# Table rows by one-hot matmul: one fp32 matmul a chunk in place of two on rounded halves

## The reference

```python
e = jnp.stack([tbl_0[ids[:, 0]], ..., tbl_25[ids[:, 25]]], axis=1)
combined = jnp.concatenate([dense[:, None, :], e], axis=1)
interactions = jnp.einsum('bfd,bgd->bfg', combined, combined)
z = jnp.concatenate([dense, interactions[:, iu, ju]], axis=1)   # iu, ju: 351 pairs
h = jnp.concatenate([z, dense], axis=1)
h = jnp.maximum(h @ W_top1 + b_top1, 0.0)
h = jnp.maximum(h @ W_top2 + b_top2, 0.0)
y = h @ W_top3
```

## Time and profile before

| | us |
|---|---|
| median of 3 runs | 196.87 |
| lowest, highest | 195.58, 198.09 |
| the profiled execution | 195.5 |
| its span in the trace | 193.7 |
| TensorE busy | 113.5 |
| VectorE, ACT, POOL busy | 75.6, 73.3, 66.7 |

### The profile page before, as it was taken

One profiled execution on the slowest core, in us unless ns is written; L12 is line 12 of the kernel. 1 busy time (PEld: TensorE's weight loads), 2 busy tenths in 40 slices (PEclk: granted clock), 3 DMA queues, 4 the chain that ended last, 5 costly groups with the idle time before them and its releaser, 6 DMA issues.

```text
span 193.7 us, 2685 instructions
## 1 busy us (share of the span) xinstructions
PE 113.5 (59%) x1038; PEld 94.6 (49%) x1038; DVE 75.6 (39%) x153; ACT 73.3 (38%) x160; POOL 66.7 (34%) x75
## 2 busy tenths in 40 slices
PE   1699300940004900100009999975799999989995
PEld 0377100720003600100007767765799898979894
DVE  3797314811100500010149799937192262014400
ACT  7864213411003001110035898448194373233512
POOL 3777837777777856777300000000000000000000
PEclk9999955596555765555555999999699999999999
DMA  5487532252211381121102740000000000000000
GB/s 189 131 266 203 169 89 60 53 177 54 56 52 48 83 234 31 53 54 54 41 0 76 250 129 0 0 3 0 12 4 6 8 0 3 0 0 5 3 0 0
DMA packets 6304, 12.58 MB, mean 65 GB/s; under 512 B 2545, under 2 KB 3157, under 8 KB 6163
## 3 DMA queue, kind: packets, MB, share of 16 engines
q1 hardware_dynamic: 3971, 7.68, 13.6%
q0 software_dynamic: 2176, 4.46, 8.6%
q10 hardware_dynamic: 144, 0.26, 0.4%
HBM read 11.27 MB, written 0.00 MB: 58 GB/s over the span
## 4 chain that ended last, share of the span: by engine, by line
PE 50%; another core or an unknown queue 33%; ACT 8%; DVE 3%; issue 3%; DMA 2%; ACTq 0%; DVEq 0%
PE ps L541 10%; PE ps L544 9%; PE ps L602 9%; PE ps L573 9%; PE ps L557 3%; PE ps L615 3%; PE ps L524 2%; ACT emb_t L383 2%; DVE z L487 2%; ACT hot L377 2%; DMA ids_i<-in_ids_dram 2%; PE ps L511 1%; ACT away L369 1%; ACT z L410 1%
## 5 line engine op out<-in xcount | busy, mean ns | idle before, releaser
L342 POOL DMA_INDIRECT rows<-in_tbl_dram,ids_i x68 | 65.9, 969 | 26.9 <-issue 24.2
L541 PE MATMUL ps<-hot,tab_hi 125*128 125x512 f32 x72 | 34.6, 481 | 55.8 <-ACT emb_t L383 55.7
L460 DVE TENSOR_SCALAR hot<-ps,row_no 125x512 fp32r<-125x512 f32 x54 | 37.7, 744 | 67.0 <-remote 39.9
L541 PEld LDWEIGHTS ps<-hot,tab_hi 125*128 125x128 f32 x72 | 17.0, 235 | 62.2 <-ACT emb_t L383 57.1
L544 PE MATMUL ps<-hot,tab_lo 125*128 125x512 f32 x72 | 33.3, 462 | 0.7 <-issue 0.7
L377 ACT ACTIVATE hot<-away 125x512 fp32r<-125x512 f32 x18 | 10.9, 627 | 43.4 <-remote 35.4
L487 DVE COPY z<-ps 32x112 f32<-32x112 f32 (+1 forms) x64 | 16.5, 258 | 15.8 <-PE ps L573 15.0
L410 ACT COPY z<-ps 32x112 f32<-32x112 f32 (+1 forms) x64 | 15.3, 239 | 13.5 <-PE ps L573 12.8
L573 PE MATMUL ps<-emb_t 128*64 128x52 f32 x512 | 17.9, 233 | 3.7 <-ACT emb_t L402 2.2
L573 PEld LDWEIGHTS ps<-emb_t 128*64 128x64 f32 x512 | 17.2, 149 | 5.1 <-ACT emb_t L402 3.1
L544 PEld LDWEIGHTS ps<-hot,tab_lo 125*128 125x128 f32 x72 | 16.8, 233 | 5.0 <-issue 1.2
(11 more groups left out here) (44 smaller groups left out, 77.4 us busy)
## 6 DMA issues: line engine op xcount, KB each, us to landing
tab<-in_tbl_dram SPq DMA_DIRECT2D x9, 448.0 KB
rows<-in_tbl_dram,ids_i POOLq DMA_INDIRECT x68
w_fold<-w_pair SPq DMA_DIRECT2D x1, 1024.0 KB
w<-in_W_top_dram SPq DMA_DIRECT2D x1, 512.0 KB
tab<-in_tbl_dram SPq DMA_DIRECT2D x9, 52.0 KB
x_rows<-in_r_dense_features_dram ACTq DMA_DIRECT2D x1, 256.0 KB, 2.8
w_x<-in_W_top_dram SPq DMA_DIRECT2D x1, 256.0 KB
h_t<-in_W_top_dram SPq DMA_DIRECT2D x1, 256.0 KB
```

The source lines that it names most:

```text
L342: pool.indirect_dma_start(out=rows[:, t, gathered.index(f), :], out_offset=None, in_=tables[f - 1], in_offset=bass.IndirectOffsetOnAxis(id ...
L460: nc.vector.tensor_scalar(hot[0:RP, k % OHB], ps[0:RP, IDV + n % 2, :], row_no[0:RP, c:c + 1], None, ALU.is_equal).then_inc(hot_dve, 1)
L541: nc.tensor.matmul(bank, tab_hi[0:RP, n % SPLIT, c], one_hot, start=c == 0, stop=False)
```

## The change

The one-hots become plain fp32, and a chunk is one fp32 matmul on the loaded table in place of two on its halves. `tab_hi`, `tab_lo`, the cast on ACT and the subtraction on VectorE are gone, and with them two semaphores. TensorE waits for the table's own load (`tab_in`). `tab` has three buffers and the one-hots sixteen; SP loads table n when all eight chunks of table n - 3 have been used. The broadcasts for table n + 2 stand ahead of the last two chunks of table n and no longer behind them.

```diff
--- before.py
+++ after.py
@@ -78,9 +78,8 @@
     ND = 2
     ACT_CHUNKS = (3, 6)
     DVE_CHUNKS = tuple(c for c in range(R8) if c not in ACT_CHUNKS)
-    OHB = 10
-    RAW = 2
-    SPLIT = 2
+    OHB = 16
+    RAW = 3
     gathered = [f for g in GROUPS for f in features(g) if f]
     assert D == P and N1 == BK and sorted(gathered + ONEHOT) == list(range(1, NF))
     assert all(tables[f - 1].shape[0] == R8 * RP for f in ONEHOT) and w1.shape[0] == 2 * D + NPAIR
@@ -162,9 +161,7 @@
         row_no = sb("row_no", [P, R8])
         neg_row = sb("neg_row", [P, R8])
         tab = sb("tab", [P, RAW, R8, D])
-        tab_hi = sb("tab_hi", [P, SPLIT, R8, D], F32R)
-        tab_lo = sb("tab_lo", [P, SPLIT, R8, D], F32R)
-        hot = sb("hot", [P, OHB, B], F32R)
+        hot = sb("hot", [P, OHB, B])
         away = sb("away", [P, 2, B])
         h1_t = sb("h1_t", [P, 2, NB, P])
         w_xb = h1_t[:, 1].rearrange("p c b -> p (c b)")
@@ -201,8 +198,6 @@
         w_x_ready = sem("w_x_ready")
         ids_bc_dve = sem("ids_bc_dve")
         ids_bc_act = sem("ids_bc_act")
-        hi_ready = sem("hi_ready")
-        lo_ready = sem("lo_ready")
         hot_dve = sem("hot_dve")
         away_ready = sem("away_ready")
         hot_act = sem("hot_act")
@@ -272,7 +267,7 @@
             def load_table(n):
                 if n >= RAW:
 
-                    sp.wait_ge(lo_ready, n - RAW + 1)
+                    sp.wait_ge(hot_used, (n - RAW + 1) * R8)
                 lines = tables[ONEHOT[n] - 1].rearrange("(p c) d -> p c d", c=R8)
                 for p0, p1 in ((0, SPREAD), (SPREAD, RP)):
                     sp.dma_start(tab[p0:p1, n % RAW], lines[p0:p1]).then_inc(tab_in[n], 16)
@@ -352,12 +347,6 @@
             nc.scalar.copy(w_pair[:].rearrange("p k n -> p (k n)"),
                            zeros[:].to_broadcast([P, NQ * N1])).then_inc(w_pair_zeroed, 1)
 
-            def split_hi(n):
-                act.wait_ge(tab_in[n], 32)
-                if n >= SPLIT:
-                    act.wait_ge(hot_used, (n - SPLIT + 1) * R8)
-                nc.scalar.copy(tab_hi[0:RP, n % SPLIT], tab[0:RP, n % RAW]).then_inc(hi_ready, 1)
-
             def build_hots(n):
                 act.wait_ge(ids_bc_act, n + 1)
                 if n == 0:
@@ -383,17 +372,13 @@
                 nc.scalar.copy(emb_t[:, :, :, ONEHOT[n]],
                                ps[:, ROT + bank_of(s), :].rearrange("p (t b) -> p t b", t=T)).then_inc(stored_act, 1)
 
-            split_hi(0)
             build_hots(0)
-            split_hi(1)
             for s in steps:
                 if s[0] == "hot":
                     n = s[2]
                     if n + 1 < NH:
                         build_hots(n + 1)
                     store_hot(s)
-                    if n + 2 < NH:
-                        split_hi(n + 2)
                 elif s[0] == "group" and stored_by_act(s):
                     act.wait_ge(group_ps, s[1] * NG + s[2] + 1)
                     copies = list(group_copies(s))
@@ -444,16 +429,9 @@
             nc.vector.tensor_copy(ids_t[:], ps[0:NF - 1, IDV + 1, :]).then_inc(ids_t_ready, 1)
             dve.wait_ge(row_no_ready, 1)
 
-            def split_lo(n):
-                dve.wait_ge(hi_ready, n + 1)
-                nc.vector.tensor_tensor(tab_lo[0:RP, n % SPLIT], tab[0:RP, n % RAW], tab_hi[0:RP, n % SPLIT].bitcast(F32),
-                                        ALU.subtract).then_inc(lo_ready, 1)
-
             def build_hots(n):
                 dve.wait_ge(ids_bc_dve, n + 1)
                 for m, c in enumerate(DVE_CHUNKS):
-                    if m == 2:
-                        split_lo(n)
                     k = n * R8 + c
                     if k >= OHB:
                         dve.wait_ge(hot_used, k - OHB + 1)
@@ -530,21 +508,17 @@
                 if s[0] == "hot":
                     n = s[2]
                     wait_bank(s)
-                    pe.wait_ge(hi_ready, n + 1)
+                    pe.wait_ge(tab_in[n], 32)
                     bank = ps[:, ROT + bank_of(s), :]
                     for c in range(R8):
+                        if c == R8 - 2 and n + 2 < NH:
+                            broadcast_ids(n + 2)
                         if c in ACT_CHUNKS:
                             pe.wait_ge(hot_act, n * len(ACT_CHUNKS) + ACT_CHUNKS.index(c) + 1)
                         else:
                             pe.wait_ge(hot_dve, n * len(DVE_CHUNKS) + DVE_CHUNKS.index(c) + 1)
-                        one_hot = hot[0:RP, (n * R8 + c) % OHB]
-                        nc.tensor.matmul(bank, tab_hi[0:RP, n % SPLIT, c], one_hot, start=c == 0, stop=False)
-                        if c == 0:
-                            pe.wait_ge(lo_ready, n + 1)
-                        nc.tensor.matmul(bank, tab_lo[0:RP, n % SPLIT, c], one_hot,
-                                         start=False, stop=c == R8 - 1).then_inc(hot_used, 1)
-                    if n + 2 < NH:
-                        broadcast_ids(n + 2)
+                        nc.tensor.matmul(bank, tab[0:RP, n % RAW, c], hot[0:RP, (n * R8 + c) % OHB],
+                                         start=c == 0, stop=c == R8 - 1).then_inc(hot_used, 1)
                 elif s[0] == "group":
                     _, t, g = s
                     feats = features(GROUPS[g])
```

## The result

The changed kernel takes 216.37 us (median of 4, 214.04 to 220.81) against 196.66 for the kernel before (now the median of 4). The ratio is 1.089, with a 95% interval of 1.077 to 1.101; it leaves disturbed runs out, and so lies a little under the ratio of the medians. The forecast was 215.2 us. The profiled execution took 214.44 us, with a span of 212.6.

A forecast was written before the change was run, and what follows sets the result against it. Late TensorE counts bound the kernel until about 100 us, then TensorE's own work. Tables +17.8, store and broadcasts +0.5, front 0, last stretch 0: +18.3 on execution 195.5 gives 213.8, plus 1.4 makes 215.2 us; range 204 to 225.

The forecast's parts named there:

- Two regimes: Until about 100 us TensorE's late counts to other engines set the pace; from 101.5 us TensorE's own work does.
- An fp32 chunk at 0.90 us: Tables behind 101.5 us: a chunk grows from 0.455 to 0.90 us, a table by 3.56, five tables by 17.8.
- Rival 4: One-hot matmuls: fp32 costs two passes, a chunk stays at 0.455 us, only the broadcasts' 0.5 counts: 197.4 us; chance 0.06.
- The slow start adds nothing: TensorE from 101.55 us: nearly 5 us of slow passes (0.42 us, not 0.23) recur unchanged, adding nothing.
- The broadcasts at 0.5 us: Broadcasts moved ahead of the last two chunks no longer hide ACT's store: about 0.5 us in all, between 0 and 1.5.
- The front adds nothing: Before 101.5 us: slower first tables are swallowed by a backlog whose end POOL sets; 0, bounds +9 or -9 us.
- paying 4 us a count: Third table, from near 40 us: each of eleven TensorE counts takes 4 us, so its last comes near 83 us.
- Loads and buffers at 0: Later table loads and SP's pair-weight loads stay hidden: 0; if cover is gone, a wait of 2 to 3 us.
- The last stretch at 0: Pair products and dense layers, the last 67.5 us, do not change: 0.
- Rivals 1 and 2: Tables before 101.5 us: front slips, up to +9, 224 us (chance 0.16); or gains a table, 206 us (0.12).
- the forecast's own case: Whole kernel: fifth table starts near 101.6 us as before, five fp32 tables behind it, 215.2 us; chance 0.58.
- Rival 3: TensorE's counts to ACT and VectorE: backlog vanishes, fifth table starts before 83.2 us, 157 us; chance 0.08.

The follow-up runs named there:

- paced gathers: Two small POOL memsets put behind each gather: 157.68 us on the changed kernel, 155.09 on the kernel before; 154.50 on the changed kernel with broadcasts moved back.
- run with short matmuls: Kernel before with two extra 16-column matmuls in each chunk, their results unused: 222.45 and 254.56 us.
- one changed line on POOL: Kernel before with POOL waiting for the group just before, not the one before that, to land ahead of each group of gathers: 158.05 us.

## Why the prediction was right

*Two regimes.* Right, and shown from both sides: with the gathers cut to a quarter, both kernels lose their idle middle, and the change costs 26.3 us in place of 19.7.

*An fp32 chunk at 0.90 us.* 0.870 measured, so a table grows from 3.64 to 6.96 us: +3.3, where the sum had +3.56, and +16.6 for five tables in place of +17.8. Rival 4 (two passes) is out: the records are 0.435 us apart and not 0.23.

*The slow start adds nothing.* Right. The fifth table took 7.41 us to its broadcasts where the sixth took 5.35, 2.1 more; the kernel before lost 2.3 in the same way.

*The broadcasts at 0.5 us.* Mis-sized. The two waits that the move opens are 0.69 and 0.90 us. From the fifth table's start to the seventh's the changed kernel takes 20.3 us and the one before 12.5, 7.8 less; two tables' chunks are 6.6 of it, so the move costs about 1.2. With the hold-up gone it is 3.2 us over five tables. It and the chunk's price were off in opposite directions: 1.2 us too much for the chunks, 0.7 too little for the broadcasts, and another 0.4 too much in the last three tables, which grew by 9.6 us where their chunks alone give 10.0. Together the stretch took 42.0 us against 43.0 in the forecast.

*The front adds nothing.* Right in its times: third table's last count near 83 us (84.95), fourth table from 83 to 94 (86.03 to 95.4), fifth near 101.6 (101.82). The step that failed is its reason, "paying 4 us a count". The runs with one and two counts a table show that fewer counts bring nothing; matmuls are finished late, and counts only report it. That the third table's last count came out right was luck. The second table's store was expected between 36 and 43 us and came at 33.51, because only the first table ran partly at the slow pace: the second one's 16 records took 7.1 us (16.99 to 24.05). From there to the third's store it took 51.4 us, more than the 43 expected and nearly twice the 27 of the kernel before. What held was the end: the fourth table's store came at 100.47 us before the change and at 100.75 after it, shortly after the last gather, as it did with one count a table (102.45). Why just two tables get through between 33 and 101 us is open; with half the matmuls three did.

*Loads and buffers at 0.* No wait for a table's load in the trace of the changed kernel behind the gathers. SP's pair loads stretched (ten of them took 13 us from 85.7), and no engine waited for them. Sixteen buffers and three tables were not tried alone.

*The last stretch at 0.* It took 1.3 us more; its first 21 us ran at a mean granted clock of 0.84 in place of 0.92. Why the clock fell there I did not test.

*Rivals 1 and 2.* The profiled execution is the forecast's own case. The four times reach from 214.0 to 220.8, and the upper two could be executions with more left behind the gathers, though a whole table more would have cost some 9 us and they lie 4 to 6 above the profiled one; there is no trace of them, so this is a guess.

*Rival 3.* It did not happen by the change alone, and it was the case with the most in it: it said 157 us for a fifth table that starts early, and with paced gathers the changed kernel takes 157.7, its pair products from 86.76 us where the rival had 86. I gave the mechanism's cure no thought because I looked for it on TensorE's side; it lay with POOL. The argument against the rival, that counts were slow even "when TensorE made none", took the idle time in TensorE's record for time in which it had nothing left to finish. The run with short matmuls speaks against that; its conclusion held all the same.

Of the rule of the Trainium skill weighed ahead ("TensorE: Matmul & The Clock Gate", the section on the per-tile semaphore tail, about 26 ns an increment): the runs with fewer counts agree with it better than my own reading did, as no cost of an increment shows in them; none of them is fine enough to measure 26 ns.

## What to carry to other kernels

Before a change to one engine's work is priced, ask which part of it stands behind a stretch whose end is set elsewhere: here four of nine tables cost nothing, and the same edit costs 20, 26, 14 or 3 us, depending on how the gathers run. A long idle stretch with a releaser that the profile calls "remote", on several engines at once and in program order of one engine's work, is a reason to slow down or cut the traffic beside it as a first experiment: one changed line on POOL took 19% off this kernel (158.05 us), two small memsets beside each gather 21%. And a small instruction moved from behind a last matmul to ahead of it costs what it used to cover; the kernel with fp32 tables, paced gathers and the broadcasts back (154.5 us) is as fast as the one with split tables and paced gathers (155.1).

## What the runs showed of the hardware that was not expected

- While indirect gathers were issued every 1.25 us, TensorE's instructions started 2.1 to 3.5 us apart, with 16 columns as with 512 (the run with short matmuls, 31.55 to 53.29 us); at 1.8 us between gathers it was not held up among the tables, at 1.45 only behind them. The way is not known. Each time of this study came with a recorded span, so it is not known either whether the hold-up is there in an execution that is not recorded. The Trainium skill ("SBUF — State Buffer", section "Who interferes with whom") says of the memory's ports that TensorE never waits on anyone there. No run here shows whether ports have a part in the hold-up; they show that TensorE is slowed while POOL's gathers run.
- A 16-column fp32r matmul is not nearly free: two of them take a chunk at the slow pace from 0.85 to 1.28 us, and in the same stretch (100 to 136 us) the granted clock's record says 1.00, while what follows a chunk's first 512-column matmul starts 0.43 us behind it, the distance at 1.2 GHz. The same shows in the first table of the kernel before: 1.00 on record from 8 to 16.3 us, and distances of 0.43 us until 14.27. There the record and the pace disagree.
- An fp32 matmul of 512 columns takes 0.870 us at 2.4 GHz, 3.8 times the 0.228 of a rounded one, and shows as two records.
